# Expert rows transposed by DMA in place of TensorE and ScalarE, in a fused attention and mixture-of-experts kernel

## The reference, cut to what matters

```
x = x + retention(layernorm(x), ctx, ctx)            # layer 0
x = x + fp8_linear(layernorm(x))
x = x + cross_attention(layernorm(x), ctx)           # layer 1, 16 heads
x = x + moe(layernorm(x))

def moe(x):                                          # 2048 tokens, 8 experts, 4 per token
    logits = x @ router_weight.T + router_bias
    w, idx = top_k(logits, 4); w = softmax(w)        # combine[token, expert]
    gate, up = split(x @ gate_up_proj[e].T + gate_up_bias[e])    # 2 x 512
    gate = minimum(gate, 7); up = clip(up, -7, 7)
    act = (up + 1) * gate * sigmoid(1.702 * gate)
    y[e] = act @ down_proj[e].T + down_bias[e]       # 256
    return sum over e of y[e] * combine[token, e]
```

## Time and profile before

| what | us |
|---|---|
| median of three runs (961.57, 963.63, 967.18) | 963.63 |
| the profiled execution, its own time | 958.41 |
| its span, first to last instruction | 956.6 |

### The profile page before, as it was taken

One profiled execution on the slowest core, in us unless ns is written; L12 is line 12 of the kernel. 1 busy time (PEld: TensorE's weight loads), 2 busy tenths in 40 slices (PEclk: granted clock), 3 DMA queues, 4 the chain that ended last, 5 costly groups with the idle time before them and its releaser, 6 DMA issues. The chain is left out here.

```text
span 956.6 us, 18496 instructions
## 1 busy us (share of the span) xinstructions
PE 786.5 (82%) x6303; PEld 488.5 (51%) x6303; DVE 630.2 (66%) x1257; ACT 480.1 (50%) x947; POOL 275.5 (29%) x258
## 2 busy tenths in 40 slices
PE   0782677779886898988877898789999999999991
PEld 0441333233432433442332326378898989899880
DVE  5545656888679777678788825647777666665541
ACT  1210310445344463346657643258887677777761
POOL 6005100310040110001000001136667576666522
PEclk9796688759998799797989779789999999999995
DMA  8431373114231062101454110434534344444322
GB/s 285 115 73 44 99 200 99 34 45 132 52 116 36 23 190 61 30 23 37 156 197 155 47 38 22 145 112 63 134 58 69 63 69 69 69 65 67 59 28 23
DMA packets 70776, 81.37 MB, mean 85 GB/s; under 512 B 10080, under 2 KB 64224, under 8 KB 70560
## 3 DMA queue, kind: packets, MB, share of 16 engines
q1 hardware_dynamic: 56864, 61.00, 21.1%
q0 software_dynamic: 13824, 19.18, 12.4%
HBM read 51.65 MB, written 28.51 MB: 84 GB/s over the span
## 5 line engine op out<-in xcount | busy, mean ns | idle before, releaser
L1855 PE MATMUL gu_ps<-xt,w 128*128 128x256 f16 (+1 forms) x1920 | 209.6, 264 | 2.8 <-ACT xt L1482 2.8
L736 ACT ACTIVATE p<-st 128x512 f32<-128x512 f32 x256 | 138.8, 595 | 139.3 <-PE st L1268 138.7
L947 DVE TENSOR_REDUCE neg_max<-sc 128x2 f32<-128x1024 f32 x128 | 156.2, 1221 | 53.9 <-PE sc L1239 53.1
L1855 PEld LDWEIGHTS gu_ps<-xt,w 128*128 (+1 forms) x1920 | 173.2, 98 | 26.6 <-issue 3.8
L1565 POOL DMA_INDIRECT out<-y,block_rows x72 | 120.1, 1668 | 105.0 <-ACT y L1518 72.5
L1869 PE MATMUL dn_ps<-w,h 128*128 (+1 forms) x864 | 101.7, 275 | 3.4 <-DVE h L1738 3.4
L1239 PE MATMUL sc<-kz,sq 48*128 48x512 f16 x256 | 59.1, 433 | 40.4 <-DVE neg_max L947 36.6
L1869 PEld LDWEIGHTS dn_ps<-w,h 128*128 128x128 f16 x864 | 84.5, 98 | 14.8 <-issue 4.5
L1555 POOL DMA_INDIRECT gx<-xr_d,block_rows x72 | 78.3, 1088 | 47.2 <-DVE block_rows L1700 20.8
L635 POOL COPY rden_rows<-rden 128x512 f32<-128x512 f32 x16 | 10.8, 676 | 278.1 <-DVE rden L968 246.9
L1729 DVE TENSOR_SCALAR up<-up 128x512 f32<-128x512 f32 x72 | 32.9, 457 | 74.8 <-ACT up L1498 73.7
(11 more groups left out here) (250 smaller groups left out, 1151.9 us busy)
## 6 DMA issues: line engine op xcount, KB each, us to landing
stack_d<-t SPq DMA_DIRECT2D x16, 256.0 KB, 2.4
sq<-stack_d SPq DMA_DIRECT2D x16, 192.0 KB, 3.7
kz<-stack_d SPq DMA_DIRECT2D x16, 192.0 KB, 4.7
sq<-stack_d SPq DMA_DIRECT2D x32, 96.0 KB, 2.3
kz<-stack_d SPq DMA_DIRECT2D x32, 96.0 KB, 2.3
raw<-in_gate_up_t SPq DMA_DIRECT2D x3, 1024.0 KB, 5.1
raw_next<-in_gate_up_t SPq DMA_DIRECT2D x3, 1024.0 KB, 6.6
ctx_pad<-in_ctx SPq DMA_DIRECT2D x4, 512.0 KB, 4.1
```

The lines of the kernel that those rows point to most:

```text
L736: act.activation(p32[:, n // 2 % RING, 2 * (n % 2) + i, :], st[:, i, :], ACT.Exp, scale=QSCALE).then_inc(s_exp, 1)
L947: dve.tensor_reduce(neg_max[:, qt, :, pair], sc[:], AX.X, ALU.max, negate=True).then_inc(m_max, 1)
L1855: ins = pe.matmul(gu_ps[:, 2 * half + g, cols], weights(i, r, wi, slice(col, col + P)), xt[:, i % 2, kd, xi, own], start=(j == 0 and kd == 0),
```

## The change

SyncE transposes the gathered rows by DMA, from gx straight into one of three buffers xt; `turn_x`, `take_x` and the PSUM tile's use for them go. Buffer i % 3 may be overwritten when gate_up of block i - 3 is done. GpSimd's gather(i) waits for the transposes of block i - 4 where it waited for `turn_x`. The expert loads move from SyncE to ScalarE's queue. The mixed blocks are blocks 17, 21, 25 and 29 in place of the last four, with `odd_halves` and `lay_halves` in turns 9 and 10. The last block, now one of a single expert, is finished by row tile: down, collect, scale and add of tile 0, then of tile 1, with the two tiles in different PSUM banks.

```
+MIXED = (17, 21, 25, 29)
+PAIR_OF = {i: k for k, i in enumerate(i for i in range(NB) if i not in MIXED)}
+HALF_OF = {i: 2 * k for k, i in enumerate(MIXED)}
-        xt = sb("xt", [P, 2, KD, 2, ROWS], F16)
+        xt = sb("xt", [P, XT, KD, 2, ROWS], F16)
...
 (sync)
-            load_expert(sp, t, late_raw[EARLY_E % 2], late_in[EARLY_E % 2], EARLY_E)
-            sp.wait_ge(x_tr, 2)
-            sp.wait_ge(rows_ok, len(GROUPS))
-            for e in range(EARLY_E + 1, E):
-                need(sp, late_lo, (e - EARLY_E - 1) * WP)
-                load_expert(sp, t, late_raw[e % 2], late_in[e % 2], e)
+            for i in range(NB):
+                sp.wait_ge(g_in[i % GX], (i // GX + 1) * 32)
+                need(sp, up_mm, 2 * (i - XT + 1))
+                for r in range(2):
+                    for k in range(KD):
+                        for hl in range(2):
+                            src = gx[:, i % GX, r, 0:D].bitcast(F16)[:, hl * D + k * P:hl * D + (k + 1) * P]
+                            sp.dma_start_transpose(xt[:, i % XT, k, hl, r * P:(r + 1) * P], src).then_inc(xt_ok[i % XT], 16)
 (scalar)
-            take_x(0)
+            load_expert(act, t, late_raw[EARLY_E % 2], late_in[EARLY_E % 2], EARLY_E)
             unit(0)
             high_half(0)
             unit(1)
-            take_x(1)
             high_half(1)
+            act.wait_ge(rows_ok, len(GROUPS))
+            load_expert(act, t, late_raw[(EARLY_E + 1) % 2], late_in[(EARLY_E + 1) % 2], EARLY_E + 1)
             for i in range(NB):
                 if i + 1 < NB:
                     unit(2 * i + 2)
-                    if i + 2 < NB:
-                        take_x(i + 2)
+                    if i == LATE_FROM + WP + 1:
+                        act.wait_ge(late_lo, WP)
+                        load_expert(act, t, late_raw[(EARLY_E + 2) % 2], late_in[(EARLY_E + 2) % 2], EARLY_E + 2)
...
 (gpsimd, gather)
-                need(pool, x_tr, i - GX + 1)
+                if i >= GX:
+                    pool.wait_ge(xt_ok[(i - GX) % XT], ((i - GX) // XT + 1) * 128)
 (gpsimd, add_rows)
-                    if r == 1 and i >= PAIRED:
+                    if r == 1 and i in HALF_OF:
                         pool.wait_ge(y_out, 32 * i + 16)
+                    if r == 1 and i == NB - 1:
+                        pool.wait_ge(y_ok, i + 2)
 (tensor, gate_up)
-                pe.wait_ge(xt_ok, i + 1)
+                pe.wait_ge(xt_ok[i % XT], (i // XT + 1) * 128)
+                if half == 0 and i == MIXED[0]:
+                    pe.wait_ge(late_lo, len(LATE_PIECES))
 (tensor, down: the last block's two tiles one after the other)
+                for its, rs in [(range(IT), (0, 1))] if i < NB - 1 else [(range(IT), (0,)), (range(IT), (1,))]:
+                    if i == NB - 1 and rs == (1,):
+                        pe.wait_ge(y_add, i)
...
 (tensor, main loop)
-                if i + 2 < NB:
-                    turn_x(i + 2)
...
+XT = 3
-LATE_FROM, HALVES_FROM = 1, 12
+LATE_FROM, HALVES_FROM = 1, 9
```

More of the change, by code:

```diff
@@ L1445, in phase_m @@
         bias_of_ok, bias_put = sem("bias_of_ok"), sem("bias_put")
-        x_tr, xt_ok = sem("x_tr"), sem("xt_ok")
+        xt_ok = [sem(f"xt_ok{i}") for i in range(XT)]
         gate_mm, up_mm = sem("gate_mm"), sem("up_mm")
@@ L1451, in phase_m, with down_bank @@
         dn_mm, y_add, y_ok = sem("dn_mm"), sem("y_add"), sem("y_ok")
-        y_out = sem("y_out")
         flat = lambda a: a[:].rearrange("p a b -> p (a b)")
         def parts(i):
-            if i < PAIRED:
+            if i in PAIR_OF:
                 return [(q, 0, slice(q * ROWS, (q + 1) * ROWS)) for q in range(2)]
             return [(q, r, slice(q * ROWS + r * P, q * ROWS + (r + 1) * P)) for q in range(2) for r in range(2)]
+        def down_bank(i, r):
+            return (i + r) % 2 if i == NB - 1 else i % 2
         block = ctx.enter_context(nc.Block())
@@ L1517, in scale_y @@
                 for r in range(2):
+                    if i == NB - 1 and r == 1:
+                        act.wait_ge(y_add, i + 2)
                     ins = act.activation(y[:, i % 2, r, :], y_raw[:, i % 2, r, :], ACT.Copy, scale=share[:, i, r:r + 1])
-                ins.then_inc(y_ok, 1)
+                    if i == NB - 1 or r == 1:
+                        ins.then_inc(y_ok, 1)
             act.wait_ge(rt, CHOOSE_STEPS)
@@ L1697, in list_rows @@
             def list_rows(i):
-                if i < PAIRED:
-                    at = slice(0, 2) if i == 0 else bass.ds(look_up(0, i, SPARE + 2 * E - 2), 2)
+                if i in PAIR_OF:
+                    at = slice(0, 2) if i == 0 else bass.ds(look_up(0, PAIR_OF[i], SPARE + 2 * E - 2), 2)
                     dve.tensor_copy(block_rows[:, i, :], rows[:, at]).then_inc(list_ok, 1)
@@ L1707, in own_hot @@
             def own_hot(i):
-                if i < PAIRED:
-                    return hot[:, i, None, :].to_broadcast([P, 2, E])
-                return half_hot[:, 2 * (i - PAIRED):2 * (i - PAIRED) + 2, :]
+                if i in PAIR_OF:
+                    return hot[:, PAIR_OF[i], None, :].to_broadcast([P, 2, E])
+                return half_hot[:, HALF_OF[i]:HALF_OF[i] + 2, :]
             def take_share(i):
@@ L1720, in put_bias @@
                 need(dve, up_ok, 2 * (i - 1))
-                n = 1 if i < PAIRED else 2
+                n = 1 if i in PAIR_OF else 2
                 dve.tensor_tensor(bias_of[:, 0:n], bias16[:].rearrange("p e j -> p j e")[:, None].to_broadcast([P, n, 8, E]),
@@ L1750, in collect @@
                     dve.wait_ge(bias_ok, 1)
[L1751 to L1756, removed]
-                else:
-                    at = [bass.ds(look_up_half(1, 2 * (i - PAIRED) + r, E - 1), 1) for r in range(2)]
-                    dve.wait_ge(dn_mm, i + 1)
-                    need(dve, y_ok, i - 1)
+                down = lambda r: dn_ps[:, down_bank(i, r), r * D:(r + 1) * D]
+                if i in HALF_OF:
+                    at = [bass.ds(look_up_half(1, HALF_OF[i] + r, E - 1), 1) for r in range(2)]
+                else:
+                    at = [slice(0, 1) if i == 0 else bass.ds(look_up(1, PAIR_OF[i], E - 1), 1)] * 2
+                dve.wait_ge(dn_mm, i + 1)
+                need(dve, y_ok, i - 1)
+                if i in HALF_OF or i == NB - 1:
                     for r in range(2):
-                        ins = dve.tensor_tensor(y_raw[:, i % 2, r:r + 1], down[:, r:r + 1], bias_d[:, at[r], :], ALU.add)
-                    ins.then_inc(y_add, 1)
+                        if i == NB - 1 and r == 1:
+                            dve.wait_ge(dn_mm, i + 2)
+                        ins = dve.tensor_tensor(y_raw[:, i % 2, r, :], down(r), bias_d[:, at[r], :].rearrange("p o d -> p (o d)"), ALU.add)
+                        if i == NB - 1 or r == 1:
+                            ins.then_inc(y_add, 1)
+                else:
+                    dve.tensor_tensor(y_raw[:, i % 2], dn_ps[:, i % 2, :].rearrange("p (r d) -> p r d", r=2),
+                                      bias_d[:, at[0], :].to_broadcast([P, 2, D]), ALU.add).then_inc(y_add, 1)
             low_one_hot(0)
@@ L1811, in look_up @@
             def look_up(i):
-                if i >= PAIRED and 2 * (i - PAIRED) not in half_regs:
-                    pe.wait_ge(half_ok, 1)
-                    s = 2 * (i - PAIRED)
+                if i in HALF_OF and HALF_OF[i] not in half_regs:
+                    pe.wait_ge(table_ok, 2)
+                    s = HALF_OF[i]
                     _, values = nc.values_load_multi_w_load_instructions(
@@ L1819, in look_up @@
                         half_regs[s + q] = values[q]
-                if 0 < i < PAIRED and i not in regs:
-                    n = min(LOADS, PAIRED - i)
+                if i > 0 and i in PAIR_OF and PAIR_OF[i] not in regs:
+                    k = PAIR_OF[i]
+                    n = min(LOADS, PAIRED - k)
                     _, values = nc.values_load_multi_w_load_instructions(
-                        table[0:1, 1, i:i + n], engines=(mybir.EngineType.PE,), min_val=0, max_val=E - 1,
+                        table[0:1, 1, k:k + n], engines=(mybir.EngineType.PE,), min_val=0, max_val=E - 1,
                         skip_runtime_bounds_check_because="counted over the experts and cut at the last one")
                     for q in range(n):
-                        regs[i + q] = values[q]
+                        regs[k + q] = values[q]
             def weights(i, r, hl, cols):
-                at = slice(0, 1) if i == 0 else bass.ds(regs[i] if i < PAIRED else half_regs[2 * (i - PAIRED) + r], 1)
+                at = slice(0, 1) if i == 0 else bass.ds(regs[PAIR_OF[i]] if i in PAIR_OF else half_regs[HALF_OF[i] + r], 1)
                 return w[hl][:, at, cols].rearrange("p o c -> p (o c)")
[L1832 to L1841, removed]
-            def gate_up(i, half):
-                pe.wait_ge(xt_ok, i + 1)
-                if half == 0 and i in FIRST_BLOCK:
```

(25 more changed lines are left out.)

14 lines of the change are left out of this document (5 added, 9 removed).

## The result

The changed kernel takes 1039.14 us (median of 4 runs, 1033.88 to 1041.18) against 962.6 us for the kernel before in the same comparison: ratio 1.0836, 95% interval 1.0785 to 1.0888. That is slower, where 939 us was forecast, and 1 us above the range. The first rival, that the transposes set the pace, is what happened. The profiled execution took 1040.5 us, its span is 1038.7.

The account below looks back on a forecast made before the run. TensorE alone was taken to pace the steady blocks, one-at-a-time row additions the end. Gains of 15.3 (transposes) + 0.3 (start) + 1.9 (mixed blocks) + 6.9 (end) = 24.4 us, from 963.6, gave 939 us; range 930 to 1038.

Parts of the forecast that it names:

- The first rival: Expert phase: SyncE's transposes set the pace once t passes 0.98 us; slower, span 647.6 + 288t; chance 0.25.
- Transposes on SyncE: Each block's 8 transposing DMAs cost 8 x 0.47 = 3.8 us of SyncE, hidden under the new 7.86 us period.
- t: Time one transposing DMA on SyncE holds up the next; taken as 0.47 us from a plain 128-partition issue.
- The bounds of 0.242 and 1.33: Limits on t in us: small SyncE issues below, an issue behind a backed-up queue above.
- tipping point, 0.98: Value of t in us below which 8 transposing issues stay under TensorE's 7.86 us period and are hidden.
- The start: Blocks 0 and 1: 3 us lost on block 0 come back before block 1; gain 0.3 us, loss near 9 at t 1.09.
- The transposes on TensorE: Steady blocks: removing TensorE's transposes saves 34 x 0.45 = 15.3 us; period falls from 8.31 to 7.86 us.
- The mixed blocks: Spread mixed blocks, each behind a paired one, should all cost 6.43 us of gate_up; gain 1.9 us, bounds 0 and 6.6.
- The cover on DVE and ScalarE: Idle time hides expert loads on ScalarE and layout steps on DVE: cost 0, at most 2.7 and 3 + 3 us.
- The tail: After the last gate_up: finishing the last block by row tile shrinks 24.7 us to 17.8; gain 6.9 us.
- The other rivals: Row additions stretch (chance 0.10), transposes half hidden (0.11), or freed time becomes other waits, no change (0.04).
- The row additions: GpSimd's loop: landings 1.5 times as long make it 8.8 us a block, median 971 us; chance 0.10.

Follow-up runs that it names:

- the eighth experiment: On the sixth experiment, DVE's late weight pieces and layout steps moved behind the clip and product of the next block's first half: 950.64 us, ratio 0.9898.
- the sixth experiment: The first experiment with the layout of the mixed blocks in turns 11 and 12 in place of 9 and 10: 952.37 us, ratio 0.9928.
- the first experiment: The changed kernel with 2 transposing DMAs a block (128 rows x 512 columns each) in place of 8 of 128 x 128: 954.08 us, ratio 0.9913.
- the fifth: The kernel before with only two transposing DMAs a block from SyncE and expert loads on ScalarE; mixed blocks stay last: 956.75 us, ratio 0.9983.

## Why the prediction was wrong

**The step that failed: "Transposes on SyncE".** I took t = 0.47 us because the plain 128-partition issue of the earlier trace rows was "the same engine moving 128 partitions by a hardware queue". The kind of DMA, not the engine or the partitions, carries the price: 1.232 us for a transposing instruction, 0.602 for a plain one on the same tile. The term t was to be the time by which one holds up the next: forecast 0.47, measured 1.275 between undisturbed issues and 1.353 on average. The bounds of 0.242 and 1.33 held the length of an issue, not this average, so the time came out 1 us above the range. The first rival's formula holds: 647.6 + 288 x 1.353 = 1037.3 against a span of 1038.7. That its upper bound came so near is luck, for 1.33 was the price of a plain issue behind others. What failed was to put half of the chance on the low end of a range whose tipping point, 0.98, lay inside it, with no row of a transposing DMA to decide.

The Trainium skill (VectorE: DVE Perf Modes, The three transpose paths) lists 1309 ns for this transpose; the issues measured here, 1.23 us long and 1.35 apart on average, lie on either side of it, and the 1032 us that it gave was close. But the 512-column instruction at 1.267 us shows that here this is the price of one instruction, not of each 128x128 piece. Another page of the Trainium skill (Advanced Engine Details and Errata, X-Bar Transpose (TRN2)) calls transposing DMAs on this chip as fast as regular ones; SyncE's 1.232 against 0.602 us says otherwise for the issue.

**The start.** The loss named for t of 1.09 was near 9 us. The term's own formula gives block 0 only 7.2 there (7 x 1.09 + 2.1 in place of 2.5), and 8.5 at the measured 1.275. From block 0's first gather (613.83 before, 615.83 after) to its first gate_up it took 17.7 us instead of 8.5, 9.2 more.

**The transposes on TensorE** were worth what was said: where nothing else waits, the period is 7.86 (the two down products of the eighth experiment above, 717.66 and 725.52).

**The mixed blocks** were mis-sized. Forecast was 4 x 1.2 = 4.8 us over paired blocks by the pieces in the earlier trace rows; by whole periods it is 5.5, the excess of 1.4 + 1.4 + 2.6 + 2.0 = 7.4 in the kernel before less the 1.9. In the sixth experiment the excess of their periods over 7.86 is 2.4 + 2.0 + 2.5 + 1.7 = 8.6, so the spread gained nothing here. Their two gate_up halves take 7.0 to 7.7 us together by the lengths in its timeline, where the first mixed block of the kernel before takes 6.75; why is open.

**The cover on DVE and ScalarE** was costed at 0 and failed once the block was shorter. With 84 idle us of 250 there seemed to be room, but a half block passes ScalarE, DVE, ScalarE and DVE in turn, and an instruction put into that chain delays it although both engines idle. The timeline of the first experiment shows it in a turn with layout steps and a late piece: ScalarE waits 2.79 us for DVE's product, TensorE then 2.08 for ScalarE, and the period is 10.1 us instead of 7.86.

```profile
721.48 0.21 DVE L1652 TENSOR_TENSOR more<-counts,consts 128x64 f32<-128x64 f32 x1
...
723.64 1.22 DVE L1754 SCALAR_TENSOR_TENSOR w<-late_raw,w 128x1024 f16<-128x1024 f32 x1
...
725.96 0.63 ACT L1506 ACTIVATE h<-prod 128x512 f16<-128x512 f32 x1 [2.79 <-DVE prod L1742]
...
727.56 2.79 PE L1860 MATMUL gu_ps<-xt,w 128*128 128x256 f16 x24 [2.08 <-ACT glu L1493]
```

Behind that chain the room is not free either: in the eighth experiment the late piece moved there kept block 6 waiting.

For the sixth experiment the 12.1 us missing can be placed. The forecast's stretch from first to last gate_up was 309.7 - 15.3 - 1.9 - 3.2 (the gap behind block 0) = 289.3 us; measured are 301.4. I set each block's period against the one before less the forecast's terms. Blocks 2 to 16, the turns of the late pieces and the layout among them, are 7.4 us over, the four mixed blocks 8.6 - 5.5 = 3.1, the other blocks from 18 on 2.6, block 0 0.5; block 1 is 1.5 under, a gain that the forecast did not have. Of the 2.6, 2.0 are the last block's alone. There block 34's down product, which stands between the two last halves, waits for DVE, a wait that the sum did not have:

```profile
925.67 1.48 PE L1877 MATMUL dn_ps<-w,h 128*128 x12 [1.65 <-DVE h L1747]
```

**The tail** was 6.9 us in the sum. After the change it shrank by 6.1, in a kernel whose other engines stood idle; at full speed by 3.3 to 3.7 (21.3 and 20.9 us in the eighth and sixth). There the last block's steps on ScalarE queue behind block 34's scaling (y), which the count of the path left out; ScalarE's timeline in the sixth:

```profile
931.17 0.91 ACT L1521 ACTIVATE y<-y_raw,share 128x256 f32<-128x256 f32 x2 [1.76 <-DVE y_raw L1775]
931.99 0.81 ACT L1493 ACTIVATE glu<-gu_ps,bias_now 128x256 f32<-128x256 f32 x2
```

**The other rivals.** The row additions did not stretch: at the end of the kernel after GpSimd waits 3.02 us for a landing, before 2.98 and 2.95. With TensorE no longer held up by the transposes, in the last blocks of the sixth experiment, it waits 3.04 to 3.35; one landing of the fifth, with 4.89, is the exception.

## What to carry to other kernels

When a new kind of DMA goes on a queue, no row of another kind prices its issue, so where the tipping point lies inside the bounds the slow side gets its full weight, and the same transfer in fewer instructions is the first thing to look for (two transposing DMAs for eight turned 1039 us into 954). Engine idle time is cover only where the moved work stands outside the chain that hands a block from engine to engine. Work that becomes faster must be followed to the ordered writes at the end, which here, in one profile, took back 3.6 of 7.5 us until the mixed blocks had been moved.

## What the runs showed of the hardware

- SyncE's price of a transposing DMA hardly depends on its width: 1.232, 1.247 and 1.267 us for 128, 256 and 512 columns of two bytes; a plain copy of 128 columns 0.602.
- 29 of the 288 issues in the kernel after took over 1.4 us (up to 2.8), together 21 us more than the others. Of these 28 overlap a 16 KB packet of the instruction queue, of the other 259 only 16. That is a coincidence in time; no run tested it.
- Whether the transposes could be shared between SyncE and ScalarE was not tried. The Trainium skill (DMA: Bandwidth & Descriptors, Silent corruption: two transposing streams in flight at once) warns that two transposing streams of one core in flight together can corrupt each other's data; no run here shows it.
